# Routing of a fused recurrent, feed-forward and mixture-of-experts kernel: the shared expert's down product in high and low parts, two tiles behind its up product

## The reference, cut to what matters

```python
def _swiglu(x, w1, w2):
    h = x @ w1.T
    x1, x2 = jnp.split(h, 2, axis=-1)
    return x1 * jax.nn.silu(x2) @ w2.T
shared_out = _swiglu(x, shared_w1, shared_w2)            # x: 2048 x 256, FFN = 768
gates = jax.nn.softmax(x @ wg.T, axis=-1)
w_topk, idx_topk = jax.lax.top_k(gates, 8)               # weights divided by their sum
# each expert takes its first 160 rows in token order ("rank < CAPACITY")
h = jnp.einsum('ech,efh->ecf', buf, expert_w1)
out = jnp.einsum('ecf,ehf->ech', x1 * jax.nn.silu(x2), expert_w2)
combined = jnp.zeros((T, H)).at[st].add(y)               # weighted rows, added back
return shared_out + combined
```

## Time and profile before

| | |
|---|---|
| median of 3 runs | 2030.68 us |
| the profiled execution's own time | 2035.27 us |
| its span | 2033.1 us |
| PE busy | 2000.0 us, 98% |
| DVE busy | 1602.5 us, 79% |
| ACT busy | 1385.7 us, 68% |
| POOL busy | 543.7 us, 27% |
| first up product of `routing` starts | 1324.16 us |
| first matmul of `experts` starts | 1441.63 us |
| an expert in the steady part | 9.0 us |

### The profile page before, as it was taken

How to read it: one execution, slowest core, us unless ns; L and a number is a source line. 1 busy time by engine, 2 the same in 40 slices (tenths; PEclk the granted TensorE clock), 3 DMA queues, 4 the chain that set the end, 5 groups by cost and what they waited for, 6 DMA issues and landing times. The chain is left out here.

```text
span 2033.1 us, 84578 instructions
## 1 busy us (share of the span) xinstructions
PE 2000.0 (98%) x34646; PEld 1829.6 (90%) x34655; DVE 1602.5 (79%) x8154; ACT 1385.7 (68%) x4138; POOL 543.7 (27%) x564
## 2 busy tenths in 40 slices
PE   9999999999999999999999999999899999999997
PEld 7899999999999999999877888876699999999997
DVE  7887888888888888888865565488688888888885
ACT  4665666666666666666555776664699888988984
POOL 0000000000000000000000000154588888888884
PEclk7988988988989889889899999999999999999998
DMA  4001000000000000000000422240699999998892
GB/s 133 4 4 46 4 4 4 4 4 4 4 4 4 4 4 4 4 4 4 4 2 34 143 84 90 90 167 19 233 311 299 305 310 300 308 312 300 307 310 34
DMA packets 55554, 213.82 MB, mean 105 GB/s; under 512 B 11578, under 2 KB 40960, under 8 KB 46976
## 3 DMA queue, kind: packets, MB, share of 16 engines
q1 hardware_dynamic: 36276, 184.41, 24.7%
q0 software_dynamic: 17408, 23.61, 5.7%
q10 hardware_dynamic: 1484, 0.40, 0.1%
HBM read 192.82 MB, written 15.57 MB: 103 GB/s over the span
## 5 line engine op out<-in xcount | busy, mean ns | idle before, releaser
L1845 POOL MEMSET cum<- 128x320 f32 x1 | 0.4, 365 | 1227.5 <-POOLq L1157 1227.5
L581 ACT ACTIVATE r_h<-bank 128x8 f32<-128x8 f32 x512 | 93.5, 183 | 262.7 <-PE bank L959 262.3
L959 PE MATMUL bank<-keep_part,Us 128*128 128x64 f16 (+2 forms) x6120 | 266.1, 189 | 0.0
L959 PE MATMUL bank<-raw,Us 128*128 128x64 f16 (+2 forms) x6132 | 264.0, 189 | 1.4 <-issue 1.4
L959 PEld LDWEIGHTS bank<-keep_part,Us 128*128 128x128 f16 x6120 | 244.0, 100 | 0.4 <-issue 0.2
L959 PEld LDWEIGHTS bank<-raw,Us 128*128 128x128 f16 x6132 | 216.7, 99 | 1.5 <-issue 1.5
L2064 POOL DMA_INDIRECT out_rows<-res,to_row x128 | 199.4, 1558 | 55.6 <-issue 27.7
L959 PE MATMUL bank<-rh_high,Us 128*128 128x32 f16 (+1 forms) x4088 | 196.4, 182 | 1.7
L959 PE MATMUL bank<-step_high,Us 128*128 128x32 f16 (+1 forms) x4088 | 192.1, 181 | 3.9 <-DVE step_high L873 0.4
L959 PEld LDWEIGHTS bank<-rh_high,Us 128*128 128x128 f16 x4088 | 142.6, 99 | 45.9 <-DVE rh_high L859 8.1
L2120 PE MATMUL bank<-second_xe_part,second_up_part 128*128 128x160 f16 x2304 | 170.5, 233 | 1.7 <-issue 1.6
(11 more groups left out here) (340 smaller groups left out, 5229.2 us busy)
## 6 DMA issues: line engine op xcount, KB each, us to landing
ring<-in_ew SPq DMA_DIRECT2D x39, 2304.0 KB
rows_then_ring<-in_ew SPq DMA_DIRECT2D x13, 2304.0 KB
inputs_and_states<-in_ew SPq DMA_DIRECT2D x12, 2304.0 KB
raw<-in_L_cond_ew SPq DMA_DIRECT2D x16, 1024.0 KB, 6.3
ctx_rows<-rows_then_ring SPq DMA_DIRECT2D x2, 1280.0 KB, 6.7
dense_w<-in_L_ffn_W SPq DMA_DIRECT2D x2, 1024.0 KB, 9.4
dense_w<-in_L_cond_sw SPq DMA_DIRECT2D x2, 1024.0 KB, 6.6
out_rows<-res,to_row POOLq DMA_INDIRECT x128
```

Source lines behind the costliest of these rows:

```text
L581: nc.scalar.activation(r, pre_of(0, q, jj), ACT.Tanh, scale=inv[0]).then_inc(s_r, 1)
L959: last = nc.tensor.matmul(pre[g][q][:, jj - n + 1:jj + 1, m, :], Us[:, g, p, k, m * P:(m + 1) * P], x[part][:, k * B:(k + 1) * B].unsqueez ...
L1845: nc.gpsimd.memset(cum[:, 0:ROW], 0.0).then_inc(s_z, 1)
```

## The change

- The shared down product of tiles 1 to 3 is taken in three products of high and low fp32r parts, as the up product is: six matmuls of 128x512 to a unit. Tile 0 keeps plain fp32. The down weights are split once, in three pieces, during tile 0 (`high_down` on ACT, `low_down` on POOL). The gated hidden values are split unit by unit: `high_gated` on ACT, and `low_gated` on POOL, or on DVE for the last four units (`LATE`). Gated values and their parts are held in rings of three units (`HELD`).
- The down product of a unit stands on PE two units behind its up product, rather than after the whole tile. The last unit of a tile stands behind the first up unit of the next one.
- The base rows are turned into banks 6 and 7, one block later than before on ACT's list; the output rows have one buffer, not two. The last block's copy out of PSUM moves into the `experts` stage.
- The lists are turned behind the last tile's first down unit, the sums of squares one unit later. The mask is turned between two down units.
- The first gather stands ahead of POOL's product of unit f = 3 of the last tile, instead of behind that of f = 4. Expert 0's rows are turned after the whole down product, and six filler matmuls follow rather than four.
- The first two gather buffers get a place of their own, so that the new parts may lie under the others.

```diff
+                def up_unit(b, f):
+                    n = b * KF + f
+                    if f == 0:
+                        pe.wait_ge(s_xhi, b + 1)
...
+                        pe.wait_ge(s_xlo, b + 1)
...
+                def down_unit(b, f):
+                    n = b * KF + f
+                    if f == 0 and b:
+                        pe.wait_ge(s_base, b * KD)
...
+                    pe.wait_ge(s_ahi, n - KF + 1)
+                    for w, a in MEET:
+                        if a:
+                            pe.wait_ge(s_alo, n - KF + 1)
+                        for d in range(KD):
+                            last = nc.tensor.matmul(down[d][:], down_parts[w][:, f, d * P:(d + 1) * P], act_part[a][:, n % HELD],
+                                                    start=(f == 0 and w == 0 and a == 0), stop=(f == KF - 1 and a == 1), skip_group_check=True)
+                    last.then_inc(s_dp, 1)
...
                 for b in range(B):
...
+                    up_unit(b, 0)
+                    if b == 1:
+                        offset()
+                    if b:
+                        down_unit(b - 1, 5)
+                    up_unit(b, 1)
+                    up_unit(b, 2)
+                    down_unit(b, 0)
+                    if last_one:
+                        turn_order()
...
+                    up_unit(b, 5)
+                    down_unit(b, 3)
...
+                    down_unit(b, 4)
+                down_unit(B - 1, 5)
+                pe.wait_ge(s_bc, (B - 1) * KD)
+                pe.wait_ge(s_got[0], 32)
...
+                keep_busy(nc, bank[0], ones_bf, idle_rows[:], 6)
...
+                first_weights(2)
+                high_gated(UNITS - 1)
+                store_base(B - 2)
+                act.wait_ge(s_tin, 1)
...
                         pool.wait_ge(s_silu, n + 1)
-                        nc.gpsimd.tensor_tensor(act_f[:, f], act_f[:, f], lin[:, n % 2], ALU.mult).then_inc(s_act, 1)
+                        nc.gpsimd.tensor_tensor(gated[:, n % HELD], gated[:, n % HELD], lin[:, n % 2], ALU.mult).then_inc(s_act, 1)
+                        if n > KF and n - 1 < UNITS - LATE:
+                            low_gated(n - 1)
...
-                        if b == B - 1 and f == KF - 2:
-
+                        if b and f == 2 and not last_one:
+                            add_base(b - 1)
+                        if last_one and f == 2:
                             pool.wait_ge(s_tok, 2)
                             pool.wait_ge(s_rows, 96)
                             gather(pool, 0)
```

More of the change, by code:

```diff
@@ L1713, in turn_mask, with offset, turn_order @@
                     last.then_inc(s_mt, 1)
+                def offset():
+                    pe.wait_ge(s_off, 1)
+                    pe.wait_ge(s_v, 32)
+                    nc.tensor.matmul(bank[6][:, 0:1], shift[:], cum[:, TH - 1:TH], start=True, stop=True).then_inc(s_off, 1)
+                def turn_order():
+                    pe.wait_ge(s_ot, 1)
+                    pe.wait_ge(s_bc, (B - 2) * KD)
+                    nc.tensor.transpose(bank[6][:, 0:P], order[:, 1, 0:P], ident[:])
+                    nc.tensor.transpose(bank[7][0:CAP - P, 0:P], order[:, 1, P:CAP], ident[:]).then_inc(s_ot, 1)
@@ new lines, in down_unit @@
+                def down_unit(b, f):
+                    n = b * KF + f
+                    if f == 0 and b:
+                        pe.wait_ge(s_base, b * KD)
+                    if b == 0:
+                        pe.wait_ge(s_act, n + 1)
+                        for d in range(KD):
+                            last = nc.tensor.matmul(down[d][:], sw2[:, f, d * P:(d + 1) * P], gated[:, n % HELD],
+                                                    start=(f == 0), stop=(f == KF - 1), skip_group_check=True)
+                        last.then_inc(s_dp, 1)
+                        return
+                    if n == KF:
+                        pe.wait_ge(s_wlo, KF + DOWN_PIECES)
+                    pe.wait_ge(s_ahi, n - KF + 1)
+                    for w, a in MEET:
+                        if a:
+                            pe.wait_ge(s_alo, n - KF + 1)
+                        for d in range(KD):
+                            last = nc.tensor.matmul(down[d][:], down_parts[w][:, f, d * P:(d + 1) * P], act_part[a][:, n % HELD],
+                                                    start=(f == 0 and w == 0 and a == 0), stop=(f == KF - 1 and a == 1), skip_group_check=True)
+                    last.then_inc(s_dp, 1)
@@ new lines, in _ @@
+                    if last_one:
+                        sum_squares()
+                    up_unit(b, 4)
+                    down_unit(b, 2)
+                    if b and not last_one:
+                        turn_base(b - 1)
+                    up_unit(b, 5)
+                    down_unit(b, 3)
+                    if last_one:
+                        turn_base(b - 1)
+                    if b == 0:
+                        turn_mask()
+                    down_unit(b, 4)
+                down_unit(B - 1, 5)
@@ L1949, in _, with low_gated @@
                     dve.wait_ge(s_tok, c + 1)
+                def low_gated(n):
+                    dve.wait_ge(s_ahi, n - KF + 1)
+                    dve.wait_ge(s_dp, n if n == UNITS - LATE else n - HELD + 1)
+                    nc.vector.tensor_tensor(act_part[1][:, n % HELD], gated[:, n % HELD], act_part[0][:, n % HELD].bitcast(F32), ALU.subtract).then_inc(s_alo, 1)
+                low_gated(UNITS - 4)
                 dve.wait_ge(s_ss, 1)
@@ L1971, in _, with first_weights @@
                 inverse_of(nc, marks, bits, MARK_INV, MARK_S, EARLY_SCALES).then_inc(s_sc, 1)
[L1972 to L1973 removed]
+                def first_weights(i):
+                    dve.wait_ge(s_whi, KF + DOWN_PIECES + i + 1)
                     split.low_weights(first_up[1], first_up[0], 0, i).then_inc(s_wlo, 1)
+                low_gated(UNITS - 3)
+                first_weights(0)
+                low_gated(UNITS - 2)
+                first_weights(1)
+                first_weights(2)
+                low_gated(UNITS - 1)
                 dve.wait_ge(s_got[0], 32)
@@ L2027, in lin_bank, with wait @@
             return bank[2 * (n % 2) + 1][:, 0:2 * CAP]
-        def wait(eng, s, n):
+        def wait(eng, s, n, first=0):
             if n > 0:
-                eng.wait_ge(s, n)
+                eng.wait_ge(s, first + n)
         with nc.Block() as block:
@@ L2187, in silu @@
                     act.wait_ge(s_pre, FIRST_PRE + n * 2 + 1)
-                    wait(act, s_mid, n - 1)
+                    wait(act, s_mid, n - 1, FIRST_MID)
                     act.wait_ge(s_sc, scale_steps(e, 3))
                     nc.scalar.activation(gate[:, n % 2], gate_bank(n), ACT.Silu, scale=split.inverse(e)).then_inc(s_silu, 1)
+                for d in range(KD):
+                    nc.scalar.activation(hist[:, d, B - 1], bank[4 + d][:], ACT.Copy).then_inc(s_block, 1)
                 for e in range(NE):
```

256 lines of the change are left out of this document (151 added, 105 removed).

## The result

The changed kernel takes **2044.48 us** (median of 3 runs, 2043.92 to 2045.78) against 2030.68 before: ratio 1.0070, 95% interval 1.0057 to 1.0084. It is slower by 0.7%. The forecast was 2029.4, and the range ended at 2034.0. The profiled execution took 2044.48 us with a span of 2042.7 (before: 2035.27 and 2033.1). The execution profiled before was 4.6 above its median, this one is at its median; so the medians differ by 13.8 us and the two profiled executions by 9.2.

The account below looks back on a forecast made before the run. The prediction took PE, busy 98% of the span, as the bound. Its terms -6.9 - 4.7 + 6.8 + 1.0 + 2.2 + 0.3 gave -1.3 us, so 2029.4 on the median's scale, range with rivals 2023.5 to 2034.0.

Parts of the forecast that it names:

- Down product: Tiles 1 to 3 on PE: three-part fp32r down product takes 8.2 us a tile instead of 10.5; -6.9 us.
- First gather: Before expert 0's rows: PE's 2.89 us wait for the gather and 1.85 of half clock go; -4.7 us.
- Borders: Two tile borders: PE waits 1.0 and 2.4 us for POOL's late low parts; +6.8 us, from 5 to 8.
- Offset: The lists' offset matmul waits for DVE's count, which meets POOL's `low_down` and `low_context`; +1.0 us, from 0 to 2.4.
- Small change: Tiles 1 and 2: ACT's copies and squares push a silu back by 1.0; +0.3 us.
- The end of the stage: Last down unit waits +0.9 for ACT and DVE; 2.6 us from last down matmul to experts, against 1.3; +2.2 together.
- Rival 3: Expert 1's gather, beside expert 3's load, lands at 1445.7 and delays DVE in the experts; +3.6 us, 2034.3; chance 0.15.
- Rival 1: Tile borders: the border waits don't come about; sum without them -8.1, 2022.6 us; chance 0.12.
- Rival 2: Start of `experts`: expert 1's idle gaps shrink by 3 with expert 3's load later; -4.3, 2026.4 us; chance 0.13.
- Rival 4: Tile borders: the waits bring the half clock, twice 1.85; +2.4, 2033.1 us; chance 0.12.

Follow-up runs that it names:

- experiment 4: Changed kernel with the low part of a tile's last unit right behind the next tile's `low_context` on POOL, at borders 1 to 2 and 2 to 3: 2038.43 us.
- experiment 7: experiment 6 with the base rows of tiles 1 and 2 turned between down units 3 and 4: 2029.69 us, ratio 0.9990 to the kernel before.
- experiment 1: Changed kernel with expert 1's gather issued right behind expert 0's: 2042.93 us, ratio 1.0064 to the kernel before.
- experiment 2: Changed kernel with the load of expert 3's weights moved from routing to the start of the experts stage: 2039.66 us, ratio 1.0044 to the kernel before.
- experiment 8: experiment 7 with the load of expert 3 in routing, issued once expert 1's gather has landed: 2030.03 us, ratio 1.0004 to the kernel before.
- experiment 11: experiment 7 with block 2's sum on DVE and expert 1's gather ahead of POOL's product of unit 23: 2030.97 us, ratio 0.9997 to the kernel before.
- experiment 9: experiment 7 with POOL's sum of block 2 back at its late place, between the products of units 22 and 23: 2031.83 us, ratio 0.9998.
- experiment 12: experiment 11 with the lists' offset matmul behind down unit 5 of tile 0 instead of ahead of it: 2029.29 us, ratio 0.9988.
- experiment 13: experiment 12 with the load of expert 3 back in routing, issued once expert 1's gather has landed: 2027.70 us, ratio 0.9985.
- experiment 3: Changed kernel with the first gather back behind POOL's product of unit f = 4 of the last tile: 2048.95 us, ratio 1.0091 to the kernel before.
- experiment 5: Changed kernel with POOL's sum of block 2 moved ahead of the first gather and its wait for the lists: 2046.54 us, ratio 1.0080.
- experiment 6: Changed kernel with the edits of experiment 2, experiment 4 and experiment 5 together: 2031.71 us, ratio 1.0006 to the kernel before.

## Why the prediction was wrong, by its own steps

The prediction had the experts 116.2 us after the first up product; they came at 127.1, and their first one took 2.2 more.

- **Down product, -6.9.** Right: a unit takes 1.37 us as forecast.
- **First gather, -4.7.** Right for the wait of 2.89, which is gone with its half clock. But the forecast had no half clock at all before expert 0's rows, and there is one, behind DVE's wait (0.51 in 1438 to 1440): what the gather gave back of the clock, 1.85, the end of the stage took again (below).
- **Borders, +6.8.** Right to 0.1: 1.03, 2.37, 1.03 and 2.36, each at the named place with the named releaser. Experiments 4 and 7 remove them one kind at a time.
- **Offset, +1.0.** 0.78: DVE's count takes 3.75 us beside POOL's `low_context`, where it took 2.29.
- **Small change, +0.3.** Too small. Tile 2 takes 1406.07 - 1376.40 = 29.67 us, where its parts and its waits add to 28.7. Each wait comes after the modelled end of the matmuls before it (4 at 1379.21 take 1.08, not 0.91), and cutting the product into units adds such seams. About 1 us in this tile; over the stage 2.2 by the remainder, which I worked out and did not test.
- **The end of the stage, +2.2: the step that failed.** The prediction followed both lists "at today's durations", and took 1.3 us more than today for what comes behind the last down unit, with 0.7 for the barrier. Both assumptions failed. DVE's subtraction took 4.67 us and not 0.69, PE waited 2.17 where 0.9 was counted (+1.3), and the half clock behind it cost 1.8 (eight transposes 1.56 for 0.79, twelve matmuls 3.26 for 2.72, the two before 1.02 for 0.57). The lists' tables added 0.44. From the end of the last down product to the experts it took 1448.94 - 1442.37 = 6.57 us instead of 2.6 (+4.0), since the barrier opens only when the gather of expert 1 has landed. In all +7.4.
- **Rival 3** had the cause of the largest part, 6.2 us: expert 1's gather beside the load of expert 3. It looked for the wait at DVE's turn in the experts, from a landing at 1445.7, and priced it at 3.0 + 1.85. The gather landed at 1448.3, and the wait stands earlier, at the barrier, which all engines pass only when the gather has landed (experiments 1, 2, 8, 11): 4.0 more than was counted, and 2.2 of half clock in the first 48 matmuls (5.72 us for 3.48). Given chance: 0.15.
- **Rivals 1 and 2** didn't come about. Every border wait is there. The second expert did shrink, from 13.1 us to 10.2, but the third grew from 9.1 to 12.5: the time moved by one expert, and the two together take 22.7 us where they took 22.2.
- **Rival 4,** half clock at the borders, came true at one border of two, for 1.4 us where it had 1.85 to a border.

The parts: 116.2 + 1.3 + 1.8 + 0.4 + 4.0 + 1.4 + 2.2 - 0.2 = 127.1, of which the 2.2 is the remainder; the half clock behind the barrier, 2.2, comes on top. The three largest terms, each read from rows, were right but for that clock. What failed is the end of the stage, twice. It took the barrier as 0.7 us whatever was in flight, and its own case left out the late gather that rival 3 had: 6.2 us. And it added up durations of a list with idle POOL beside it: 3.1 us, though the earlier trace rows showed a DVE instruction lengthened by a meeting with POOL. The Trainium skill, SBUF — State Buffer, "Who interferes with whom", says that the engine that issues first keeps the pair of SBUF ports that DVE and GpSimd share for the whole instruction, and the other one blocks. The trace agrees with the blocking, and goes further: one DVE instruction stood over the rest of one POOL instruction and two whole ones (4.67 us in the changed kernel and in experiments 2, 4 and 9, 4.62 in experiment 1). The prediction weighed that rule for the count of the lists and not for the end of the stage, where POOL's list had just lost its gaps.

## What to carry to other kernels

When a change takes the gaps out of one engine's list, go through every instruction of the other engine that can meet it there, and price it by the whole run without a gap and not by one instruction. Before a stage's barrier, look at what the last indirect DMA shares its queues with: in this program the barrier ends with its landing, so a big load belongs behind that landing, and then as early as it can. And follow a gain to the place where the steady part begins: from experiment 7 to 12, 4.8 us won ahead of the experts were 1.3 at the fourth one, and 3.9 once the load moved too (experiment 13).

## What the runs showed of the hardware that I had not expected

- A DVE subtraction of two SBUF tiles was not let in between large POOL instructions that follow one another without a gap. It ended 0.55 us after the last of them: 4.67 us beside the rest of one and two whole ones, 1.36 or 1.37 where it met one (experiments 3 and 5), 0.69 alone. POOL's 128x1 copies, which follow on that last one at 1435.88 without a gap, didn't keep it out. A 128x64 `tensor_scalar` of 0.25 took 2.31 beside a POOL sum (experiment 7).
- The barrier between two stages opened 9.3 us after the issue of a gather with a 2304 KB load beside it (1439.46 to 1448.77 on POOL), and 3.4 us after it without one (1433.71 to 1437.13, experiment 7), though no instruction ahead of it waits for that gather. Each time that is 0.5 us after the landing.
- The same wait of 2.37 us at a border was followed by the half clock at both borders in experiment 3, at one in the changed kernel and in experiment 5, and at none in experiments 1 and 2. That of 2.5 us for the tables was followed by it in experiments 5, 7 and 8 and not in 6. What decides it stays open.
